# The up part of the expert tiles as three products of rounded parts, with the weights split ahead of time by GpSimd

## The chip, the cores and the metric

The kernel runs on one core of one Trainium2 chip, as one launch. The metric is the device time in microseconds, the median of three runs. The profile comes from one execution of its own; times in it are counted from the first instruction.

## The reference

A model of eight stages works on 1,024 tokens with 256 columns each. Each stage adds its result, computed from the layer-normed tokens, to the stream `x`. All values are fp32.

```python
x = x + L0_attn_a(ln(x))   # stage 0: recurrent attention in segments, 16 heads
x = x + L0_ffn(ln(x))      # stage 1: experts and a shared part, 704 wide
x = x + L0_attn_b(ln(x))   # stage 2: causal attention, 16 heads of 128
x = x + L0_ffn(ln(x))      # stage 3: weights of stage 1
x = x + L1_attn_a(ln(x))   # stage 4
x = x + L1_ffn(ln(x))      # stage 5: experts and a shared part, 176 wide
x = x + L1_attn_b(ln(x))   # stage 6
x = x + L1_ffn(ln(x))      # stage 7: weights of stage 5

def ffn(x):                # E = 8 experts, two for each token
    w, chosen = top_k(softmax(x @ gate_w.T), 2)
    y = sum(w_e * ((silu(x @ gate_e) * (x @ up_e)) @ down_e) for the two chosen e)
    return y + shared(x)   # silu(x @ g) * (x @ u) @ d
```

The inner width of an expert is 176.

## The kernel before

Tokens lie on the partitions, 128 in a tile, and `res.x` holds the stream for the whole launch. The stages follow one another, each with its own buffers and its own program for each of the five engines; nothing of a stage begins before the stage ahead of it has ended on all engines. What an engine does in a stage is an order written out by hand, with waits on semaphores.

**Products in fp32.** There are two kinds. A plain `matmul` of fp32 operands shows as two records of TensorE. `product` takes both operands as a rounded part `hi` (type float32r, made by a copy) and a rest `lo` (value minus `hi`), and adds up three matmuls, hi x hi, hi x lo and lo x hi, one record each. The shared parts, the router and the projections use `product`; the expert tiles use plain matmuls.

**An expert stage** (`ffn_stage`). After the norm and the routing, which gives every token its two experts and places, 23 tiles (`TILES`) of 128 rows each are gone through; each tile belongs to one expert, whose number TensorE's sequencer reads (`find_owner`, line 558). SP loads the weights of all 8 experts at the start of the stage, in 8 DMAs of 128 rows with 1,216 columns: 704 for the gate and up part, and 512 for the down part, of which 88 rows are used. In stages 1 and 3, three of the six loads of shared weights are queued behind them. For each tile:

- GpSimd gathers 128 rows of the normed tokens (`gather`, line 384), 8 tiles ahead, and scatters the result (`scatter`, line 391). Its order is 8 gathers, then scatter i and gather i+8 in turn.
- TensorE: `turn_x` transposes the rows (514), `expert_up` multiplies them by the 352 gate and up columns, in two halves of 128 rows of weights (527), `turn_h` transposes h (538), `expert_down` multiplies it by the down part (551).
- ScalarE copies the transposed rows (`x_out`, 659), applies silu (665), copies the transposed h (`h_out`, 671) and the result (`y_out`, 677).
- VectorE multiplies silu by the up part (`h_of_tile`, 882).

Before the loop VectorE works out the weights of the tokens (lines 856 to 876), in stages 5 and 7 with a diagonal matrix of weights (872); in stages 1 and 3 it also adds a first run of the shared part (`add_shared`). After the loop TensorE does the rest of the shared part, SP waits for the last scatter and loads the scattered rows back, and VectorE adds them.

The order on TensorE in the loop is, for tile i: `turn_x(i+3)`, `find_owner(i+2)`, `expert_up(i+2)`, `expert_down(i)`, `turn_h(i+1)`.

**GpSimd in stages 0 and 2.** Both stages go over four groups of four heads. GpSimd splits the weights of a group in hi and lo: a copy by adding zero (lines 2645 and 1055) and a subtraction (2648 and 1058), 128x1024 each. In stage 0 (`recurrent_stage`) it splits seven such blocks at the start of a group and is then idle until TensorE has done the group's output products. In stage 2 (`wide_stage`) the splits of a group are spread over the group; those of the output weights wait for TensorE's output products.

## Time and profile before

| | us |
|---|---|
| median of three runs | 1646.33 |
| lowest and highest | 1643.37, 1650.38 |
| span of the profiled execution, first to last instruction | 1607.0 |
| device time of the profiled execution | not listed; the runs lie 36 to 43 above its span |
| TensorE busy in it | 1491.0 (93%) |
| VectorE busy | 909.4 (57%) |
| ScalarE busy | 752.9 (47%) |
| GpSimd busy | 412.6 (26%) |

TensorE's granted clock was full nearly throughout (mean 0.995). The stages begin at about 0 (stage 0), 416 (1), 549 (2), 953 (3), 1085 (4), 1241 (5), 1345 (6) and 1499 us (7). In the views, PE is TensorE, PEld its weight loads, PEldq its sequencer, DVE is VectorE, ACT ScalarE, POOL GpSimd, and SPq or POOLq a queue that issues DMAs. The time of a matmul record includes its passage through the pipeline, so the cost of one in a row of many is the distance between two starts. L527 is line 527 of the kernel. A row of windows gives the stretch, its length, the busy time and count of PE, PEld, DVE, ACT and POOL, the granted clock, the DMA share and the GB/s.

### The profile page before, as it was taken

The numbers are of one execution on the slowest core, as the hardware profiler recorded it, in microseconds if no ns is written. First come the engines' busy times: TensorE is split into PE (matmuls) and PEld (weight loads), VectorE is DVE, ScalarE is ACT, GpSimd is POOL, SyncE is SP. The second block draws the span as 40 slices with busy tenths as digits, with TensorE's granted clock in tenths as the row PEclk, the third lists the DMA queues.
The fourth block names the chain that finished last, engine by engine and source line by source line (L and its number), as shares of the span: only waits on it lengthen the run. The fifth ranks groups of instructions, "written<-read, shape, count | busy, mean of one in ns | idle before, by whom it ended". The sixth has DMA issues, their size and how long they took to land. (4 is left out here: it accounts for less than half of the span.)

```text
span 1607.0 us, 28561 instructions
## 1 busy us (share of the span) xinstructions
PE 1491.0 (93%) x10462; PEld 1100.8 (68%) x10462; DVE 909.4 (57%) x1972; ACT 752.9 (47%) x1872; POOL 412.6 (26%) x328
## 2 busy tenths in 40 slices
PE   6999999998899899999999999998998998999898
PEld 4778877777677677778777767765555676533576
DVE  5766576666651656566565557147665515477712
ACT  5564656655334334343434433433443343677242
POOL 2706125040136142031211012622000461100173
PEclk9999999999999999999999999999999999999999
DMA  4103010010513421000010024221000523000533
GB/s 152 37 1 92 2 66 28 21 33 2 221 44 96 162 59 47 1 13 33 13 33 0 1 84 165 86 93 48 2 1 24 209 92 114 1 1 1 188 100 124
DMA packets 43143, 99.99 MB, mean 62 GB/s; under 512 B 7184, under 2 KB 21904, under 8 KB 42896
## 3 DMA queue, kind: packets, MB, share of 16 engines
q1 hardware_dynamic: 33040, 70.05, 12.9%
q0 software_dynamic: 9984, 28.32, 5.4%
q8 instruction: 79, 1.29, 0.3%
q14 instruction: 40, 0.33, 0.1%
HBM read 80.00 MB, written 18.35 MB: 61 GB/s over the span
## 5 line engine op out<-in xcount | busy, mean ns | idle before, releaser
L882 DVE TENSOR_TENSOR s_h_e<-s_bank,s_silu_e 128x176 f32<-128x176 f32 x92 | 31.2, 341 | 182.1 <-ACT s_silu_e L665 182.1
L527 PE MATMUL s_bank<-s_expert_w,s_xe 128*128 x368 | 124.8, 462 | 1.8 <-ACT s_xe L659 1.1
L384 POOL DMA_INDIRECT s_xg<-normed_rows,s_from_row x92 | 93.1, 1011 | 106.8 <-DVE s_from_row L790 79.9
L144 POOL TENSOR_SCALAR ln_var<-ln_moments 128x4 f32<-128x4 f32 x16 | 4.1, 255 | 450.7 <-DVE ln_moments L129 261.7
L391 POOL DMA_INDIRECT expert_rows<-s_y,s_to_row x92 | 91.1, 990 | 89.5 <-ACT s_y L677 71.5
L2645 POOL TENSOR_TENSOR s_w_hi<-s_w_raw,zero 128x1024 fp32r<-128x1024 f32 x25 | 55.6, 2222 | 211.0 <-PE s_memory L80 188.0
L1251 ACT ACTIVATE s_scratch<-s_bank,s_neg_max 128x128 f32<-128x128 f32 (+3 forms) x128 | 67.3, 528 | 84.9 <-DVE s_neg_max L1341 84.7
L551 PE MATMUL s_bank<-s_expert_w,s_he 88*128 x368 | 95.4, 381 | 4.9 <-ACT s_he L671 4.9
L1341 DVE TENSOR_REDUCE s_neg_max<-s_bank 128x1 f32<-128x128 f32 (+3 forms) x128 | 59.5, 487 | 55.9 <-PE s_bank L1141 55.7
L1139 PE MATMUL s_bank<-s_k,s_q 128*128 128x128 f32 (+3 forms) x256 | 88.6, 441 | 1.5 <-DVE s_v L1336 0.8
L551 PEld LDWEIGHTS s_bank<-s_expert_w,s_he 88*128 88x128 f32 x368 | 69.1, 189 | 29.7 <-issue 6.9
L1055 POOL TENSOR_TENSOR s_w_hi<-s_w_raw,zero 128x1024 fp32r<-128x1024 f32 x11 | 22.7, 2060 | 254.6 <-PE s_bank L80 122.8
L2331 ACT ACTIVATE s_exps<-s_bank,s_rms 128x512 f32<-128x512 f32 x128 | 76.7, 696 | 19.9 <-PE s_bank L2211 19.9
L78 PE MATMUL s_bank<-xn_t_hi,s_w_hi 128*128 128x512 f32 x192 | 80.9, 421 | 1.3 <-DVE xn_t_lo L211 1.2
L527 PEld LDWEIGHTS s_bank<-s_expert_w,s_xe 128*128 128x128 f32 x368 | 62.7, 190 | 22.6 <-issue 3.2
L1158 PE MATMUL s_bank<-s_probs_t,s_v 128*128 128x512 f32 (+3 forms) x256 | 74.6, 434 | 1.7 <-ACT s_probs_t L1259 1.7
L80 PE MATMUL s_bank<-xn_t_hi,s_w_lo 128*128 128x512 f32 x192 | 75.7, 394 | 0.0
L79 PE MATMUL s_bank<-xn_t_lo,s_w_hi 128*128 128x512 f32 x192 | 75.6, 394 | 0.0
L1259 ACT ACTIVATE s_probs_t<-s_bank 128x128 f32<-128x128 f32 (+3 forms) x128 | 49.0, 438 | 52.4 <-PE s_bank L1152 52.4
L86 PE MATMUL s_bank<-zeros 128*128 128x512 bf16 x256 | 64.0, 392 | 9.3 <-PEq L254 3.9
L1351 DVE TENSOR_SCALAR s_scratch<-s_scratch,s_row_sum 128x128 f32<-128x128 f32 (+3 forms) x128 | 67.8, 529 | 4.5
L1158 PEld LDWEIGHTS s_bank<-s_probs_t,s_v 128*128 128x128 f32 x256 | 47.5, 189 | 30.5 <-issue 17.2
(398 smaller groups left out, 4291.0 us busy)
## 6 DMA issues: line engine op xcount, KB each, us to landing
s_expert_w<-in_experts SPq DMA_DIRECT2D x32, 608.0 KB, 13.5
s_w_raw<-in_wa_o SPq DMA_DIRECT2D x16, 512.0 KB, 3.5
s_yg<-expert_rows SPq DMA_DIRECT2D x32, 256.0 KB, 4.3
s_raw<-in_shared SPq DMA_DIRECT2D x16, 384.0 KB, 6.1
normed_rows<-s_ln_xn POOLq DMA_DIRECT2D x8, 512.0 KB, 9.5
s_w_raw<-in_wa_k SPq DMA_DIRECT2D x4, 512.0 KB, 3.8
s_w_raw<-in_wa_v SPq DMA_DIRECT2D x4, 512.0 KB, 3.5
s_w_raw<-in_wa_q SPq DMA_DIRECT2D x4, 512.0 KB, 4.3
```

The source lines that it names most:

```text
L78: pe.matmul(out, sh, mh, start=first, stop=False, skip_group_check=True)
L79: pe.matmul(out, sh, ml, start=False, stop=False, skip_group_check=True)
L80: return pe.matmul(out, sl, mh, start=False, stop=last, skip_group_check=True)
L384: pool.indirect_dma_start(out=xg[:, i % XG_RING, :], out_offset=None, in_=x_rows[:, :], in_offset=bass.IndirectOffsetOnAxis(ap=from_row[:, ...
L391: pool.indirect_dma_start(out=y_rows[:, :], out_offset=bass.IndirectOffsetOnAxis(ap=to_row[:, i:i + 1].bitcast(U32), axis=0), in_=y[:, i % ...
L527: last = pe.matmul(u_bank[i % 2][:, 0:2 * INTER], xe[:, i % 2, x], expert_of(P, i, w), start=c == 0, stop=c == DC - 1, skip_group_check=True)
L551: last = pe.matmul(y_bank[i % 2][:, 0:D], he[0:IHALF, i % 2, h], expert_of(IHALF, i, w), start=c == 0, stop=c == 1, skip_group_check=True)
L1139: pe.matmul(to, q[:, b, h * S + r * P:h * S + (r + 1) * P], k[:, b, h, 0:(r + 1) * P], start=r == UNIT_ROWS[u][0], stop=False, skip_group_ ...
L1158: last = pe.matmul(o_bank[:, j * P:S], v[:, b, j, h * DH:(h + 1) * DH], probs_t[:, j, j * P:S], start=j == 0, stop=j == TB - 1, skip_group ...
L1251: act.activation(probs[:, h % 2, r, 0:(r + 1) * P], score_bank(h, r), ACT.Exp, bias=neg_max[:, 4 * h + r:4 * h + r + 1], accum_out=row_sum ...
L1351: dve.tensor_scalar(mine, mine, one, None, ALU.mult).then_inc(probs_done, 1)
L2331: act.activation(exps[:, s % 2, g, :], s_bank[g][:], ACT.Exp, scale=rms[:, b, 1, j:j + 1]).then_inc(exp_done, 1)
```

## The change

The up part of an expert tile becomes `product`, with rounded parts of the transposed rows (`xe_hi`, copied by ScalarE, and `xe_lo`, subtracted by VectorE in `low_x`) and of the expert's weights. The down part stays a plain matmul. The expert weights' parts come from DRAM: a new class `ExpertSplit` lets GpSimd load a piece of the weights, split it, and store both parts, in stage 0 for stages 1 and 3 (16 pieces of 352 columns, four behind each group's own splits), and in stage 2 for stages 5 and 7 (8 pieces of 704 columns, two before the loop over the groups and two in each of three groups ahead of the split of the output weights; that loop is written out now). Each expert stage then loads three blocks for each expert, hi, lo and the down part, in 24 DMAs. The order of TensorE, ScalarE and VectorE in the loop is changed: transposes of the rows run four tiles ahead, the up part three. Some buffers share addresses now (`first_of`).

```diff
@@ ffn_stage @@
-        e = sb("expert_w", [P, N_EXP, EXP_COLS])
+        e_hi, e_lo = sb("expert_w_hi", [P, N_EXP, EXP_DOWN], F32R), sb("expert_w_lo", [P, N_EXP, EXP_DOWN], F32R)
+        e_down = sb("expert_w_down", [IHALF, N_EXP, 2 * D])
...
+        xe_hi, xe_lo = sb("xe_hi", [P, 2, D], F32R), sb("xe_lo", [P, 2, D], F32R)
...
                     for one in range(N_EXP):
-                        sp.dma_start(e[:, one, :], experts[one]).then_inc(e_loaded, 16)
+                        for to, part in zip((e_hi, e_lo), experts[1:]):
+                            sp.dma_start(f32(to[:, one, :]), part[one]).then_inc(e_loaded, 16)
+                        sp.dma_start(e_down[:, one, :], experts[0][one, 0:IHALF, EXP_DOWN:EXP_COLS]).then_inc(e_loaded, 16)
...
             def expert_up(i):
-                pe.wait_ge(xe_done, i + 1)
+                pe.wait_ge(xe_lo_done, i + 1)
...
-                    last = pe.matmul(u_bank[i % 2][:, 0:2 * INTER], xe[:, i % 2, x], expert_of(P, i, w),
-                                     start=c == 0, stop=c == DC - 1, skip_group_check=True)
+                    last = product(pe, u_bank[i % 2][:, 0:2 * INTER], (xe_hi[:, i % 2, x], xe_lo[:, i % 2, x]),
+                                   [part_of(part, i, w) for part in (e_hi, e_lo)], c == 0, c == DC - 1)
...
             turn_x(2)
             expert_up(1)
+            turn_x(3)
             turn_h(0)
+            find_owner(2)
+            expert_up(2)
             for i in range(TILES):
-                if i + 3 < TILES:
-                    turn_x(i + 3)
-                if i + 2 < TILES:
-                    find_owner(i + 2)
-                    expert_up(i + 2)
-                expert_down(i)
+                if i + 4 < TILES:
+                    turn_x(i + 4)
                 if i + 1 < TILES:
                     turn_h(i + 1)
+                expert_down(i)
+                if i + 3 < TILES:
+                    find_owner(i + 3)
+                    expert_up(i + 3)
...
@@ scalar @@
             for i in range(TILES):
-                if i + 3 < TILES:
-                    x_out(i + 3)
                 if i + 2 < TILES:
                     silu_of(i + 2)
-                y_out(i)
+                if i + 4 < TILES:
+                    x_out(i + 4)
                 if i + 1 < TILES:
                     h_out(i + 1)
+                y_out(i)
...
@@ vector @@
+            def low_x(i):
+                dve.wait_ge(xe_hi_done, i + 1)
+                dve.tensor_tensor(xe_lo[:, i % 2, :], xt_bank[i % 2][:, 0:D], f32(xe_hi[:, i % 2, :]), ALU.subtract).then_inc(xe_lo_done, 1)
+
+            low_x(0)
+            low_x(1)
             if early:
                 for b in range(4):
                     add_shared(b, 1)
+            h_of_tile(0)
+            low_x(2)
+            h_of_tile(1)
+            low_x(3)
             for i in range(TILES):
-                h_of_tile(i)
+                if i + 2 < TILES:
+                    h_of_tile(i + 2)
+                if i + 4 < TILES:
+                    low_x(i + 4)
...
@@ wide_stage, gpsimd @@
-            with pool.Fori(1, GROUPS) as i:
-                split(i, (0, 1, 2))
+            if by_run:
+                for n in range(2):
+                    expert_split.piece(pool, n, n, 0, n == 0)
+            for i in range(1, GROUPS):
+                split(i, (0, 1))
+                if by_run:
+                    for n in range(2):
+                        expert_split.piece(pool, 2 * i + n, 2 * i + n, 0)
+                split(i, (2,))
                 move_q(i)
+            if by_run:
+                expert_split.end(pool, N_EXP)
...
@@ recurrent_stage, gpsimd @@
-            groups(pool, group)
+            for G in range(GROUPS):
+                group(G, G < GROUPS - 1)
+                for n in range(4 * G, 4 * G + 4):
+                    expert_split.piece(pool, n, n // 2, n % 2 * E_PART, n == 0)
+            expert_split.end(pool, 2 * N_EXP)
...
+class ExpertSplit:
...
+    def piece(self, pool, n, expert, at, first=False):
...
+        if not first:
+            pool.wait_ge(self.stored, 32 * n)
+        pool.dma_start(f32(self.lo[:]), of(self.experts)).then_inc(self.loaded, 16)
+        pool.wait_ge(self.loaded, 16 * n + 16)
+        pool.tensor_tensor(self.hi[:], f32(self.lo[:]), self.res.zero[:].broadcast_to([P, self.columns]), ALU.add).then_inc(self.hi_done, 1)
+        pool.wait_ge(self.hi_done, n + 1)
+        pool.tensor_tensor(self.lo[:], f32(self.lo[:]), f32(self.hi[:]), ALU.subtract).then_inc(self.lo_done, 1)
+        pool.dma_start(of(self.parts[0]), f32(self.hi[:])).then_inc(self.stored, 16)
+        pool.wait_ge(self.lo_done, n + 1)
+        pool.dma_start(of(self.parts[1]), f32(self.lo[:])).then_inc(self.stored, 16)
```

## Rows read from the trace of the kernel before

**Rows 1.** Timeline of TensorE, stage 1: start, us, engine, line, out<-in, count
```profile
486.30 1.35 PE L527 MATMUL s_bank<-s_expert_w,s_xe 128*128 x4
487.48 1.03 PE L551 MATMUL s_bank<-s_expert_w,s_he 88*128 x4
488.35 0.38 PE L538 MATMUL s_bank<-ident,s_h_e 128*88 128x128 f32 x2
...
488.79 1.35 PE L527 MATMUL s_bank<-s_expert_w,s_xe 128*128 x4
```

**Rows 2.** Groups by line, 480 to 505: count | busy us, mean ns | idle before
```profile
L677 ACT ACTIVATE s_y<-s_bank 128x256 f32<-128x256 f32 x10 | 3.8, 384 | 5.5 <-PE s_bank L551 5.5
...
L882 DVE TENSOR_TENSOR s_h_e<-s_bank,s_silu_e 128x176 f32<-128x176 f32 x10 | 3.4, 342 | 21.5 <-ACT s_silu_e L665 21.5
```

**Rows 3.** Timeline of GpSimd, stage 1, with idle time before and its releaser
```profile
474.28 1.01 POOL L391 DMA_INDIRECT expert_rows<-s_y,s_to_row  x1 [19.23 <-ACT s_y L677]
475.59 0.96 POOL L384 DMA_INDIRECT s_xg<-normed_rows,s_from_row  x1 [0.30 <-issue]
476.85 1.00 POOL L391 DMA_INDIRECT expert_rows<-s_y,s_to_row  x1 [0.30 <-ACT s_y L677]
...
527.76 0.97 POOL L391 DMA_INDIRECT expert_rows<-s_y,s_to_row  x1 [0.99 <-ACT s_y L677]
```

**Rows 4.** Timeline of TensorE in stages 1 and 2, products of rounded parts
```profile
446.32 0.39 PE L80 MATMUL s_bank<-xn_t_hi,s_w_lo 128*128 128x512 f32 x1
446.55 0.39 PE L78 MATMUL s_bank<-xn_t_hi,s_w_hi 128*128 128x512 f32 x1
...
638.23 0.28 PE L78 MATMUL s_bank<-xn_t_hi,s_wq_hi 128*128 x1
...
638.94 1.02 PE L1139 MATMUL s_bank<-s_k,s_q 128*128 128x512 f32 x2
```

**Rows 5.** Line 558, reading of a tile's owner: ns min/median/max, first and last start
```profile
L558 PEldq TENSOR_LOAD <-s_owner x92: 294/300/541, 463.5 to 1579.6; - x92
```

**Rows 6.** DMA issues of the page: count, KB each, median us to landing
```profile
normed_rows<-s_ln_xn POOLq DMA_DIRECT2D x8, 512.0 KB, 9.5
...
s_xg<-normed_rows,s_from_row POOLq DMA_INDIRECT x92, 2.8
```

**Rows 7.** Timelines of TensorE, VectorE and GpSimd at the loop's start, stage 7
```profile
1526.62 1.38 PE L527 MATMUL s_bank<-s_expert_w,s_xe 128*128 x4
...
1527.98 1.22 DVE L872 TENSOR_TENSOR s_weight_diagonal<-ident,s_token_w 128x1024 f32<-128x1024 f32 x1
...
1528.13 1.90 POOL L384 DMA_INDIRECT s_xg<-normed_rows,s_from_row  x1 [0.30 <-issue]
```

**Rows 8.** SP's queue in stage 1; busy time by windows (DMA, GB/s last), stage 7
```profile
418.76 4.82 SPq L359 DMA_DIRECT2D s_expert_w<-in_experts  x8
...
1518.00:1520.00 2.00, 0.64 (x10) 0.36 (x10) 1.91 (x2) 0.00 (x0) 0.00 (x0) 1.00 1.02 423
```

**Rows 9.** Timeline of ScalarE, stage 1, rounding of a later load of shared weights
```profile
446.79 0.83 ACT L619 ACTIVATE s_w_hi<-s_raw 128x768 fp32r<-128x768 f32 x1
```

**Rows 10.** Timeline of GpSimd, stage 0, first split of a group
```profile
134.39 1.89 POOL L2645 TENSOR_TENSOR s_w_hi<-s_w_raw,zero 128x1024 fp32r<-128x1024 f32 x1 [64.01 <-PE s_memory L80]
136.36 2.41 POOL L2648 TENSOR_TENSOR s_w_lo<-s_w_raw,s_w_hi 128x1024 fp32r<-128x1024 f32 x1
```

**Rows 11.** Line 3009 of VectorE: ns min/median/max; windows of two splits, stage 2
```profile
L3009 DVE SCALAR_TENSOR_TENSOR s_sigma_kt<-s_exp_part,s_positive x32: 668/692/716, 23.3 to 314.2; 128x512 f32<-128x512 f32 x32
L3009 DVE SCALAR_TENSOR_TENSOR s_sigma_qt<-s_exp_part,s_positive x32: 676/1509/2719, 39.8 to 350.4; 128x512 f32<-128x512 f32 x32
...
613.00:618.00 5.00, 3.58 (x14) 1.91 (x12) 4.93 (x6) 1.16 (x4) 4.24 (x2) 1.00 0.00 0
709.00:714.00 5.00, 5.00 (x22) 3.28 (x21) 4.14 (x7) 1.51 (x4) 4.41 (x2) 1.00 0.00 0
```

More of the change, by code:

```diff
@@ L36 @@
 XG_RING, Y_RING = 8, 8
+E_PART = EXP_DOWN // 2
 AT_ORDER = P
@@ L256, in ffn_stage, with first_of @@
         sb = lambda what, shape, dt=F32: ctx.enter_context(nc.sbuf_tensor(f"{name}_{what}", shape, dt))
+        def first_of(what, shape):
+            with nc.sbuf_tensor(f"{name}_{what}", shape, F32) as first:
+                return first
         banks = [ctx.enter_context(nc.psum_tensor(f"{name}_bank{i}", [P, HALF], F32)) for i in range(8)]
@@ L3147, in _, with __init__, end @@
             groups(dve, group)
+class ExpertSplit:
+    def __init__(self, nc, ctx, sem, name, res, experts, parts, columns):
+        sb = lambda what, dt: ctx.enter_context(nc.sbuf_tensor(f"{name}_{what}", [P, columns], dt))
+        self.res, self.experts, self.parts, self.columns = res, experts, parts, columns
+        self.hi, self.lo = sb("e_hi", F32R), sb("e_lo", F32R)
+        self.loaded, self.hi_done, self.lo_done, self.stored = (
+            sem("e_raw_loaded"), sem("e_hi_done"), sem("e_lo_done"), sem("e_stored"))
+    def piece(self, pool, n, expert, at, first=False):
+        cols = slice(at, at + self.columns)
+        of = lambda whole: whole[bass.ds(expert, 1), :, cols].rearrange("a p n -> (a p) n")
+        if not first:
[8 more added lines that the diff above has]
+        pool.dma_start(of(self.parts[1]), f32(self.lo[:])).then_inc(self.stored, 16)
+    def end(self, pool, n):
+        pool.wait_ge(self.stored, 32 * n)
 class Residual:
@@ L3207, in build_program @@
         t = {**t, "x_mid": nc.dram_tensor("x_mid", (SEG, SEGS // 2, 2, B, D), F32, kind="Internal").ap()}
+        for n in range(2):
+            t[f"experts{n}_parts"] = [nc.dram_tensor(f"experts{n}_{part}", (N_EXP, P, EXP_DOWN), F32, kind="Internal").ap()
+                                      for part in ("hi", "lo")]
         rows = [nc.dram_tensor("normed_rows", (TOK, D), F32, kind="Internal").ap(),
@@ L3216, in build_program @@
             if kind == "L0_ffn":
-                ffn_stage(nc, name, res, t["shared0"], t["experts0"], t["gate0"], t["routing"], rows, True, False, "both" if n > 1 else "moments", None)
+                ffn_stage(nc, name, res, t["shared0"], [t["experts0"], *t["experts0_parts"]], t["gate0"], t["routing"], rows, True, False, "both" if n > 1 else "moments", None)
             if kind == "L0_attn_b":
@@ L3224, in build_program @@
             if kind == "L1_ffn":
-                ffn_stage(nc, name, res, t["shared1"], t["experts1"], t["gate1"], t["routing"], rows, False, True, "both" if n > 1 else "", out if n == len(stages) - 1 else None)
+                ffn_stage(nc, name, res, t["shared1"], [t["experts1"], *t["experts1_parts"]], t["gate1"], t["routing"], rows, False, True, "both" if n > 1 else "", out if n == len(stages) - 1 else None)
         nc.clear_and_free_semaphores(Semaphores.past.pop())
```

35 lines of the change are left out of this document (19 added, 16 removed).

## The prediction

> **What bounds the kernel now.** I read the timeline of TensorE inside an expert loop first, because all that the change can speed up lies there. There are four such loops (stages 1, 3, 5 and 7), of 23 tiles each. The reader sees one tile after another with no idle time on TensorE: up part from 486.30 to 487.48 (1.18 us), down part to 488.35 (0.87), the two pairs of transposes to 488.79 (0.44), and the next up part begins [rows 1]. So a tile costs 2.49 us, and TensorE alone sets it: ScalarE has four instructions of at most 384 ns in that time, VectorE one of 342 ns [rows 2]. The second engine to look at is GpSimd: in its timeline scatter, gather and scatter start at 474.28, 475.59 and 476.85, that is 2.57 us for a pair [rows 3]. That is more than a tile of TensorE; it does not bind only because 8 gathers are made ahead, so that 15 pairs and then 8 single scatters are left. From the first to the last scatter are 527.76 - 474.28 = 53.5 us.
>
> **The up part.** Two plain products of 352 columns show now as four matmul records, 0.295 us each. They become six products of rounded parts. No row shows rounded parts at 352 columns, but there are rows on both sides: 512 columns start 0.23 us apart, 256 columns 0.118 (six of them from 638.23 to 638.94) [rows 4]. Between them 352 columns give 0.16 us, six 0.96 us. The rows at 256 columns are addressed through a loop register, as the expert's weights are, so the address costs nothing there. Bounds: 0.95 (in proportion to 512 columns) and 1.18 (nothing gained). I take 0.96: 0.22 us less in a tile, 2.27 us. TensorE's sequencer also reads the owner of a tile (300 ns) [rows 5], now behind the down part; that part's eight queued instructions hide it. Uncovered it would cost 0.3 us in a tile.
>
> **The new order.** The transposes run four tiles ahead and the up part three, so every wait inside an iteration is for work of the iteration before. At the end of the loop the last down parts then follow each other directly: 0.96 + 0.22 + 0.87, then 1.09, then 0.87, which is 4.0 us for the last three tiles.
>
> **But GpSimd then ends last.** First to last scatter cannot take less than 15 pairs of 2.57 and 7 singles of 1.3: 47.7 us. TensorE alone would take 19 tiles of 2.27 and those 4.0: 47.1. The gathers add a little. A gather lands 2.8 us after its issue [rows 6], so gather i+8 is there 1.3 + 2.8 + 2.57 i after the first scatter's start. TensorE asks for it at 7.2 + 2.27 i (four tiles, 9.1, less the 1.9 from that transpose through down part and copy to a scatter). At i = 14 it comes 1.1 us late. I take 48.0 us from first to last scatter: 5.5 us less in a stage, 22.0 in four. Bounds: 6.4 (TensorE alone) and 4.7 (both delays in full).
>
> **The rounded x.** VectorE gets one subtraction of 256 columns in a tile. It reads one operand from PSUM, as the 342 ns product of 176 columns does; an estimate from that is 0.4 us. VectorE is then busy for 0.75 of 2.27 us. Queued behind the subtraction's wait for ScalarE is the product h of the next tile, which TensorE needs an iteration later: no cost inside the loop. At its start there is one. In stages 5 and 7 the first subtraction stands behind the whole weighting of the tokens, which ends with the diagonal at 1527.98 + 1.22 = 1529.2; now the first up part runs at 1526.62 [rows 7]. It will start 3.0 us later. Part of this comes back: three up parts are shorter by 0.22, and GpSimd's early gathers, one of them 1.90 us long [rows 7], now still hold TensorE there. Bounds 0.7 and 3.0; I take 1.4, nearer to the lower, as the following tiles will find their gathers landed. In stages 1 and 3 two subtractions stand ahead of the adding of the shared part: 0.25 each, between 0 and 0.8. Together 3.3 us.
>
> **The loads.** 8 DMAs of 608 KB become 24 of together 7,040 KB, 2.23 MB more. SP issues 8 in 4.82 us, so 24 take 14.5; transfers ran at 423 GB/s up to 1520 [rows 8], so the last part lands 5.3 us later, at about 1525.4. From there to the first subtraction (owner, transpose, copy) is some 1.5 us, 1526.9: hidden behind the same 1529.2. If it lands after 1527.7, each microsecond is lost twice (stages 5 and 7). In stages 1 and 3 the loads of more shared weights are queued behind on SP; the first now goes out at 418.76 + 14.5 = 433.2, lands by 442.7 even with the slowest landing below, and ScalarE takes it at 446.79 [rows 9]. Hidden.
> The Trainium skill (DMA: Bandwidth & Descriptors, section "Why a DMA increments its semaphore by 16 and not by 1") says that a DMA is spread over the largest number of engines up to 16 that divides its rows, so the down parts with 88 rows would use 11. No row here shows such a DMA. By that rule eleven engines carry 0.49 MB each instead of 0.31, and the last part lands at an estimated 1527.0, which leaves the sum as it is, with 0.7 us of cover.
>
> **The splitting on GpSimd.** 16 pieces in stage 0, 8 in stage 2. A piece is three DMA issues, two landings one after another (load, then the stores before the next piece), a rounding copy and a subtraction. At 1024 columns those two take 1.89 and 2.41 us [rows 10]; in proportion 1.5 us for 352 columns, 3.0 for 704. A landing takes between 2.8 us (a gather) and 9.5 (the normed rows, stored by GpSimd while the experts load) [rows 6]. With three issues of about 0.9 a piece is between 10 and 23 us; I take 11, as little else is loaded in stage 0. Four pieces, 44 us, lie in a gap of 64.0 us [rows 10]: hidden. Behind them on GpSimd are the next group's splits, needed half a group later.
> What is not hidden is that GpSimd and VectorE hinder each other. The same instruction of VectorE takes 692 ns as sigma_k, when GpSimd is idle, and 1509 (median) as sigma_q, when GpSimd splits [rows 11]. From 613 to 618, while GpSimd split, TensorE was busy for 3.58 of 5 us; from 709 to 714, in the same split, for all 5 [rows 11]. The new pieces are 24 us of such work in each of the two stages. Bounds: 0, and 8 (1.42 lost for each 4.24 us of splitting, all through stage 2) plus 6 in stage 0, 14. I take 2, as most stretches are like the later one.
> The Trainium skill (GPSIMD Engine Reference, section "Specifications") says that the two engines share SBUF interfaces, with contention for VectorE instructions in a two-port mode or with two SBUF inputs. The trace agrees (1509 against 692 ns). By that rule the splits pay, and the new subtraction, with one input in PSUM, leaves the gathers alone; this speaks for the 2 us and against the second rival.
>
> **The sum.** -22.0 + 3.3 + 2 = -16.7 us. The profiled execution's span goes from 1607.0 to 1590.3. Its own device time is not listed; the three runs lie 36 to 43 us above its span, the median 39.3, and nothing in the change touches that part. So 1646.3 - 16.7 = 1629.6, about **1630 us**. Unchanged means within 0.5%, 1638.1 to 1654.6.
>
> **The rivals.**
> *The splits collide with the attention stages.* The 3.58 of 5 us speak for it, the later stretch against. At 8 to 14 us instead of 2 the time is 1636 to 1642. Chance 0.10.
> *The gathers collide with the new subtraction*; this one ends slower. A gather issued beside VectorE's late work took 1.90 us instead of 0.96 [rows 7, 3]. If each pair of the loop took x more, GpSimd would set the loop at 47.7 + 15 x. From x = 0.39 the loop gains nothing; at the 0.94 seen it takes 61.8, 8.3 us more than now, four times, with the 5.3 on top: 1685 us. Against it: the h product of today, also with one operand in PSUM, runs beside pairs of 2.57 us. Chance 0.04.
> *The pieces overrun stage 0.* Decides from 16 us a piece, when four no longer fit into the 64.0. At 23 us each gap is overrun by 28; the last one has nothing behind it that could absorb it: 1658 us. Chance 0.03.
> *The weights land late in stages 5 and 7.* Decides at 1527.7. At 1530 it costs 2.3 us twice: 1634. No row shows loads in 88 rows of 2 KB, so 0.08.
> *The six products are little faster than the four*, since each weight load of about 190 ns shows: 1.14 in a tile, 50.7 in the loop, 1641 us. Against it stand the 0.118 us of [rows 4], with a load for each. Chance 0.03.
> My forecast has 0.72, between 1622 and 1637.
>
> **How the numbers follow.** 1630 is the forecast's own. The range 1621 to 1641 takes in the loop at its best (-25.6 + 1.4, no collisions: 1622), the late weights, the last rival and most of the first; outside are the second, the third and the worst of the first. Faster by over 0.5%: 0.72 + 0.08 + a third of the first rival, 0.83. Unchanged: the rest of that and the last rival, 0.10. Slower: the second and third, 0.07.
>
> **What would show it.** Right: a tile of 2.27 us with an up part of 0.96; near 48 us from first to last scatter; the first up part of stage 7 some 3 us behind its place; no wait of stage 0 for a split. Wrong: an up part near 1.14; pairs over 2.9 us; TensorE waiting for the expert weights; stages 0 and 2 longer by more than 4 us together.

## The result, and the profile after

The changed kernel takes 1667.78 us (median of four runs, 1662.52 to 1675.05) against 1646.07 us for the kernel before; the ratio is 1.0135, with a 95% interval of 1.0104 to 1.0167. It is slower by 21.7 us, where the prediction had it 16.7 us faster.

The first thing to read is the cores' view. It gives the span and the mean granted clock of TensorE, here of the kernel after and then of the kernel before run once more (its device time was 1649.98 us):

```profile
core 0: 1665.8 us, clock 0.974
```

```profile
core 0: 1648.2 us, clock 0.993
```

Device time and span lie 1.7 to 1.8 us apart. The span of 1607.0 that stood ahead of the prediction came from an execution some 37 us quicker than those timed, and of the 39 us that the prediction took to lie between span and device time, all but 1.8 lie inside the span of a usual execution. So the profile after is compared below with the second profile of before, the usual one.

**The tile on TensorE** [rows 1], in the timeline of the kernel after, stage 1:

```profile
502.08 1.03 PE L561 MATMUL s_bank<-s_expert_w_down,s_he 88*128 x4
502.75 0.51 PE L79 MATMUL s_bank<-s_expert_w_hi,s_xe_hi 128*128 x1
503.10 0.33 PE L80 MATMUL s_bank<-s_expert_w_lo,s_xe_hi 128*128 x1
...
503.75 0.32 PE L81 MATMUL s_bank<-s_expert_w_hi,s_xe_lo 128*128 x1
503.91 0.38 PE L525 MATMUL s_bank<-ident,s_xg 128*128 128x128 f32 x2
504.13 0.38 PE L549 MATMUL s_bank<-ident,s_h_e 128*88 128x128 f32 x2
504.35 1.03 PE L561 MATMUL s_bank<-s_expert_w_down,s_he 88*128 x4
505.03 0.51 PE L79 MATMUL s_bank<-s_expert_w_hi,s_xe_hi 128*128 x1
506.17 0.38 PE L525 MATMUL s_bank<-ident,s_xg 128*128 128x128 f32 x2
508.29 0.42 PE L549 MATMUL s_bank<-ident,s_h_e 128*88 128x128 f32 x2 [1.74 <-issue]
510.93 2.07 PE L561 MATMUL s_bank<-s_expert_w_down,s_he 88*128 x4 [2.22 <-ACT s_he L684]
513.09 0.49 PE L80 MATMUL s_bank<-s_expert_w_lo,s_xe_hi 128*128 x1
513.38 0.49 PE L81 MATMUL s_bank<-s_expert_w_hi,s_xe_lo 128*128 x1
```

One tile takes 504.35 - 502.08 = 2.27 us, the predicted number. The products are 0.16 us apart. But from 506.17 on TensorE stands still for most of 5 us, and then the products are 0.29 us apart: the granted clock was at half (1.2 GHz) from 509.2 to 516.0. What was missing is seen on ScalarE (timeline, idle time before each instruction in brackets):

```profile
503.29 0.39 ACT L690 ACTIVATE s_y<-s_bank 128x256 f32<-128x256 f32 x1 [0.58 <-PE s_bank L561]
507.54 0.32 ACT L678 ACTIVATE s_silu_e<-s_bank 128x176 f32<-128x176 f32 x1 [3.87 <-PE s_bank L81]
508.98 0.38 ACT L672 ACTIVATE s_xe_hi<-s_bank 128x256 fp32r<-128x256 f32 x1 [1.12 <-remote]
510.41 0.38 ACT L684 ACTIVATE s_he<-s_bank 88x256 f32<-88x256 f32 x1 [1.04 <-remote]
```

The silu at 507.54 waited for the up part that TensorE had ended at 503.75 + 0.32 = 504.07. Its semaphore was raised at 507.52, 3.4 us late; that of the transposes begun at 503.91 at 508.96, 4.7 us after their end, and that of the transposes of h behind them at 510.39, 5.9 us after theirs. In the execution of 1607.0 us the signals that ScalarE waits for in the loops are all raised within 0.02 us of the end. TensorE meanwhile went on to the next tile until it needed ScalarE's answer. So TensorE's work was on time and its signals were not. There are such places in every expert loop of every usual execution, the kernel before included, and none in the execution of 1607.0 us. The same rows as [rows 3], line of the scatters (ns min/median/max, first and last start), stage 1, after and then before in its second profile:

```profile
L402 POOL DMA_INDIRECT expert_rows<-s_y,s_to_row x23: 968/997/1011, 480.4 to 538.6; - x23
```

```profile
L391 POOL DMA_INDIRECT expert_rows<-s_y,s_to_row x23: 970/997/1010, 474.0 to 535.3; - x23
```

That is 58.2 us from first to last scatter after, 61.3 before, where the execution of [rows 3] had 53.5 and the prediction 48.0. The loop did get shorter. What got longer is the way to it. Busy time by windows in stage 7 after (the last three numbers are clock, DMA share and GB/s), to be held against the 423 GB/s of [rows 8]; below them TensorE and VectorE at the loop's start [rows 7]:

```profile
1558.00:1560.00 2.00, 1.39 (x14) 0.80 (x15) 1.36 (x7) 0.00 (x0) 0.00 (x0) 1.00 1.05 324
1564.00:1566.00 2.00, 0.00 (x0) 0.00 (x0) 1.79 (x9) 0.00 (x0) 1.69 (x2) 1.00 0.83 248
1568.00:1570.00 2.00, 0.00 (x0) 0.00 (x0) 0.00 (x0) 0.00 (x0) 1.62 (x2) 0.50 0.76 263
1574.00:1576.00 2.00, 0.57 (x2) 0.29 (x2) 0.00 (x0) 0.00 (x0) 0.00 (x0) 0.50 0.03 12
```

```profile
1566.62 1.23 DVE L886 TENSOR_TENSOR s_weight_diagonal<-ident,s_token_w 128x1024 f32<-128x1024 f32 x1
1575.43 0.66 PE L525 MATMUL s_bank<-ident,s_xg 128*128 128x128 f32 x2 [12.06 <-DMA s_expert_w_down<-in_experts]
1576.54 0.42 DVE L901 TENSOR_TENSOR s_xe_lo<-s_bank,s_xe_hi 128x256 fp32r<-128x256 f32 x1 [8.69 <-ACT s_xe_hi L672]
```

The diagonal behind which the subtraction was to stand is done at 1567.85. The weights land at 1574.1 (the end of their last packet; all landings are read so), and TensorE waits 12.06 us for them; the loop then begins at half the clock. From 12 us after the start of the stage on, all loads ran at some 330 GB/s, the last ones at 250. In stages 1 and 3 the shared weights queued behind the expert weights went out at 440.57 instead of the estimated 433.2, and TensorE waited for them (7.0 us in the page, behind the rest `s_w_lo`: 2.3 in stage 1 and 4.7 in stage 3).

Where the usual spans part, from the timelines (SP's first load of a stage is its start):

| kernel, stages 1 / 3 / 5 / 7 | first scatter after the start, us | first to last scatter, us |
|---|---|---|
| before, span 1607.0 | 57.8 / 56.6 / 34.3 / 34.8 | 53.5 / 53.5 / 52.9 / 53.5 |
| before, usual, 1648.2 | 57.7 / 56.1 / 34.5 / 34.7 | 61.3 / 62.6 / 63.1 / 64.2 |
| after, 1665.8 | 62.5 / 63.1 / 45.1 / 46.6 | 58.2 / 58.2 / 58.3 / 61.5 |

The loops gave 15.1 us back in all, the later starts cost 34.3, stage 0 cost 1.7; the rest of the 17.6 us is -3.3.

### The profile page after: what moved, and what is told of

It reads as the page before. It is cut to its first block and busy times, and to the rows that moved or that the text cites. A ratio compares the mean times of both kernels' runs of the same rounds, so it can differ in the third digit from the quotient of the medians.

```text
span 1665.8 us, 29369 instructions
## 1 busy us (share of the span) xinstructions
PE 1502.3 (90%) x10646; PEld 1139.7 (68%) x10646; DVE 942.6 (57%) x2064; ACT 752.7 (45%) x1872; POOL 502.8 (30%) x448
## 5 line engine op out<-in xcount | busy, mean ns | idle before, releaser
L561 PE MATMUL s_bank<-s_expert_w_down,s_he 88*128 x368 | 102.3, 404 | 10.2 <-ACT s_he L684 8.9
L1380 DVE TENSOR_REDUCE s_neg_max<-s_bank 128x1 f32<-128x128 f32 (+3 forms) x128 | 59.6, 487 | 55.8 <-PE s_bank L1180 55.6
L79 PE MATMUL s_bank<-s_expert_w_hi,s_xe_hi 128*128 x184 | 78.1, 425 | 3.3 <-DVE s_xe_lo L901 3.3
L561 PEld LDWEIGHTS s_bank<-s_expert_w_down,s_he 88*128 88x128 f32 x368 | 66.5, 201 | 20.2 <-issue 13.1
L1933 DVE TENSOR_REDUCE s_neg_max<-s_pair 128x2 f32<-128x1024 f32 (+3 forms) x64 | 51.5, 821 | 25.0 <-PE s_pair L1707 24.2
```

The costliest lines, as they stand in the source:

```text
L79: pe.matmul(out, sh, mh, start=first, stop=False, skip_group_check=True)
L561: last = pe.matmul(y_bank[i % 2][:, 0:D], he[0:IHALF, i % 2, h], part_of(e_down, i, slice(c * D, (c + 1) * D)), start=c == 0, stop=c == 1, ...
```

## The experiments

**The kernel before again**, unchanged.

> The kernel before once more, unchanged, to see where its device time and its span part. The prediction took the 39 us between the span of 1607.0 us and the median of 1646.3 as something that lies around the span. In the trace of the changed kernel the span (1665.8) and the device time (1667.5) are 1.7 us apart, so that reading is in doubt. Theory: a usual execution of the kernel before has a span of about 1644 us, and the 37 us more than in the profile shown are in the four expert loops, as waits for signals of TensorE that come late (first to last scatter 60 us or more instead of 53.5). Rival: the span is 1607 again, the loops take 53.5, and 39 us lie outside the span.

Device time 1649.98, span 1648.2. The four loops take 37.9 us more than in the first profile, of 41.2 us in the span. The theory holds: what the prediction counted as lying outside is time inside the loops, behind late signals; in the first profile none of them is late.

**The splitting alone**: the kernel before with the pieces of `ExpertSplit` in stages 0 and 2; `ffn_stage` is that of before.

```diff
+    for n in range(4 * G, 4 * G + 4):
+        expert_split.piece(pool, n, n // 2, n % 2 * E_PART, n == 0)
+expert_split.end(pool, 2 * N_EXP)
```

> The kernel before with the splitting of the expert weights by GpSimd in stages 0 and 2 added and nothing else: the parts are stored, but the expert stages load and use the plain weights as before. Theory (the cost of the change lies in the expert stages): 0 to 4 us above the kernel before. Rival (the splits collide with the attention stages): 8 to 14 us above it. In the two traces at hand stage 0 grew by 1.5 us and stage 2 shrank by 3.1.

1652.07 us, ratio 1.0001 (0.9979 to 1.0024). It costs nothing that can be measured; the interval, 3.5 us less to 4.0 us more, shuts out the rival, but not the 2 us of the prediction.

**The loads alone**: the kernel before with three loads for each expert and plain products.

```diff
-    sp.dma_start(e[:, one, :], experts[one])...
+    for to in (e_up, e_again):
+        sp.dma_start(to[:, one, :], experts[one][:, 0:EXP_DOWN])...
+    sp.dma_start(e_down[:, one, :], experts[one][0:IHALF, EXP_DOWN:EXP_COLS])...
```

> The kernel before with the 24 loads of the changed kernel instead of its 8: the columns of the up part are loaded twice (into two tiles; the second is not used) and the down part in 88 rows, and the products stay plain, in the order of before. Theory (the loads cost what the loop gained): the weights land 10 us later than the loop of before needs them in stages 5 and 7, and the late loads of shared weights cost some us in stages 1 and 3: 20 to 30 us above the kernel before. Rival (late signals inside the loop, or the rounded parts, cost the time): 0 to 8 us above it.

1673.08 us, ratio 1.0125 (1.0085 to 1.0164). First scatters 59.6, 59.1, 47.1 and 47.6 us after the starts, loops as before. The loads alone cost about what the whole change does.

**Down parts over 128 rows.**

```diff
-    e_down = sb("expert_w_down", [IHALF, N_EXP, 2 * D])
+    e_down = sb("expert_w_down", [P, N_EXP, 2 * D])
-    sp.dma_start(e_down[:, one, :], experts[0][one, 0:IHALF, EXP_DOWN:EXP_COLS])...
+    sp.dma_start(e_down[:, one, :], experts[0][one, :, EXP_DOWN:EXP_COLS])...
```

> The changed kernel, but the down part of each expert is loaded over 128 partitions instead of 88 (the 40 added rows are not used). In stages 5 and 7 the weights of the changed kernel land at about 1295 and 1574 us, 34 us after SP's first load of them. Theory 1 (a load of 88 rows uses 11 of the 16 DMA engines, which end last): the last part lands 3 to 5 us earlier in each stage, and the time falls by 6 to 10 us, to about 1659. Theory 2 (it is the bytes and the short rows of 2,816 and 2,048 bytes, moved at 332 instead of 423 GB/s, that make the loads late): 0.7 MB more are moved, the last part lands where it did or up to 1 us later, and the time is 1666 to 1672.

1648.43 us, ratio 0.9974 (0.9953 to 0.9994): all of the loss is gone, though 0.7 MB more are moved in each expert stage. By the two ratios that is some 26 us; the medians lie only 19 apart, but they were taken beside runs of the kernel before that differ by 6. In stages 5 and 7 the weights land 29.8 and 30.0 us after the start instead of 34.3 and 35.6, and in stages 1 and 3 the first scatter is back at 58.3 and 56.8. In stage 7 a window 21 us after the start has 413 GB/s, where the one of the kernel after had 324:

```profile
1545.00:1547.00 2.00, 2.00 (x11) 0.93 (x10) 1.87 (x7) 0.74 (x2) 0.55 (x1) 1.00 1.05 413
```

The direction is that of theory 1; the gain is well above the 6 to 10 us that it named, so its reason needed a test of its own.

**96 rows**, a number that 16 divides.

```diff
-    sp.dma_start(e_down[:, one, :], experts[0][one, 0:IHALF, EXP_DOWN:EXP_COLS])...
+    sp.dma_start(e_down[:, one, :], experts[0][one, 0:96, EXP_DOWN:EXP_COLS])...
```

> The changed kernel with the down part loaded over 96 partitions: more rows than the 88 of the change by 8, but a number that 16 divides. In the changed kernel the 8 loads of 88 rows left 40 small packets fewer than the 128-row loads (568 against 608 in the same stretch), which is 11 instead of 16 for each load. Theory (the number of DMA engines that a load is spread over makes the difference): as the 128-row loads or slightly sooner, weights landed 30 us after the start of stages 5 and 7, 1645 to 1651. Rival (the number of rows, and the share of partitions that are written, makes it): near the 88 rows, 34 to 35 us, 1660 to 1668.

1668.46 us, ratio 1.0085 (1.0057 to 1.0113); landed after 35.8 and 34.6 us. Stage 7 of the kernel after, of 128 and of 96 rows, in the DMA view:

```profile
DMA packets 4347, 10.58 MB, mean 278 GB/s; under 512 B 568, under 2 KB 696, under 8 KB 4344
```

```profile
DMA packets 4707, 11.24 MB, mean 296 GB/s; under 512 B 608, under 2 KB 736, under 8 KB 4704
```

```profile
DMA packets 4451, 10.71 MB, mean 282 GB/s; under 512 B 608, under 2 KB 736, under 8 KB 4448
```

The 40 small packets fewer fit 8 loads of 88 rows spread over 5 engines less each; with 96 rows none is missing. Yet with 96 rows the weights of stages 5 and 7 land as late. So the number of engines is not the cause of the late landing: theory 1 falls. (The time is some 14 us above the kernel before by its ratio, between the two others: in stage 1 the first scatter comes after 58.6 us, not 62.5.) What goes with the landing is the duration of a packet: in stage 7 those of 2,816 bytes took 118 ns on average beside 128-row loads, 136 beside 88 rows, 146 beside 96.

**No down loads, and down loads last.** In the first the down product takes other columns of the loaded weights; in the second the order of SP's loads alone is changed (the diff is the second's).

```diff
     for one in range(N_EXP):
         for to, part in zip((e_hi, e_lo), experts[1:]):
             sp.dma_start(f32(to[:, one, :]), part[one])...
+    for one in range(N_EXP):
         sp.dma_start(e_down[:, one, :], experts[0][one, 0:IHALF, EXP_DOWN:EXP_COLS])...
```

> The changed kernel with the loads of the down part left out: the down products take other columns of the loaded weights, so the output is not the reference's. What the two parts of the up weights take by themselves: 5.8 MB. Theory (partial loads, of 88 or 96 of 128 rows, slow the packets of the loads beside them: the mean packet of 2,816 bytes took 118 ns beside 128-row loads, 136 beside 88 rows, 146 beside 96): packets of 118 ns or less, the weights land 24 to 26 us after the start of stages 5 and 7, and 8 loads of 88 rows cost about 10 us where their bytes are worth 4; the time is 1636 to 1645. Rival (the many 2,816-byte loads are slow by themselves): packets of 130 ns and more, 28 us and later, 1645 to 1655.

> The changed kernel with its 88-row loads, but all 16 loads of the up parts go first and the 8 down parts after them. Theory (the partial loads slow what runs beside them): the up parts land by 26 us, the 88-row loads alone after them by 31 to 32, and the time is 1648 to 1657. Rival (the 88 rows cost the same in any order, as 11 engines carry them): 34 to 36 us and 1660 to 1668.

Windows of stage 7, without down loads and then with them last:

```profile
1545.00:1547.00 2.00, 2.00 (x10) 1.40 (x10) 1.73 (x9) 1.57 (x3) 0.00 (x0) 1.00 1.04 406
1549.00:1551.00 2.00, 0.64 (x13) 0.46 (x13) 1.81 (x2) 0.00 (x0) 0.00 (x0) 1.00 1.04 415
```

```profile
1549.00:1551.00 2.00, 1.31 (x20) 0.83 (x19) 1.39 (x4) 0.00 (x0) 0.00 (x0) 1.00 1.04 413
1555.00:1557.00 2.00, 0.00 (x0) 0.00 (x0) 1.86 (x7) 0.00 (x0) 1.69 (x2) 1.00 0.79 267
```

By themselves the loads of the parts run at 406 to 415 GB/s, with packets of 117 ns in both runs; the 88-row loads alone run at about 260. The landing is at 24.4 us without them and at 31.0 with them last, instead of 35.6 mixed in. So the partial loads slow the loads beside them, as the theory had it. The times are 1647.45 us (ratio 0.9995, 0.9970 to 1.0020) and 1658.01 (1.0046, 1.0016 to 1.0075), the first 2 us and the second 1 us above the bounds named. The second hangs on one run of ten that took 2839.64 us; without it the median is 1656.7, inside. As to the first: without down loads the weights are no longer last, and the loop of stages 5 and 7 waits for the rounded x. There the first up part runs 30.0 us after the start against 27.1 in the usual run of before, the 3.0 us later that the prediction had, and the first scatter is 3.8 to 4.3 us later. TensorE in stage 7, without down loads:

```profile
1560.59 0.65 PE L79 MATMUL s_bank<-s_expert_w_hi,s_xe_hi 128*128 x1 [2.37 <-DVE s_xe_lo L899]
```

The Trainium skill (DMA: Bandwidth & Descriptors, section "The descriptor swizzle") says that in a transfer to 128 partitions each engine writes one port of SBUF; for other shapes it points to the rule for the number of engines. A guess from that is that with 88 or 96 rows engines write to ports that other engines use too, beside the full loads; the 136 and 146 ns against 118 would fit, but no run shows the ports.

**Longer rows**: the two parts side by side in memory (5,632-byte rows), and then the down part copied beside them too (7,680-byte rows, one load for each expert); the diff is the first's.

```diff
-    for to, part in zip((e_hi, e_lo), experts[1:]):
-        sp.dma_start(f32(to[:, one, :]), part[one])...
+    sp.dma_start(f32(e_parts[:, one, :]), experts[1][one])...
```

> As the run with 128-row down loads, and besides the two parts of the up weights stand side by side in memory and come in one load of 5,632-byte rows for each expert (16 loads instead of 24, the same bytes). Theory (short rows move at 332 GB/s, the 4,864-byte rows of before at 396 to 423): the last weights land some 3 us earlier in each expert stage, about 27 us after the start of stages 5 and 7 instead of 30, and the time is 1636 to 1643. Rival (the number of bytes and what else is stored and gathered then set the landing, not the rows): the landing stays at 30 us and the time at 1646 to 1651.

> As the run before, and the down part too is copied beside the two parts while the experts are split (one more DMA of GpSimd, memory to memory, for each expert), so that 8 loads of 7,680-byte rows bring all weights. Theory (rows): another 1 to 2 us earlier in each expert stage, 1630 to 1640 in all. Rival: no earlier than in the run before, or the copies make stages 0 and 2 longer; 1640 to 1650.

1648.62 and 1648.38 us (ratios 1.0019, 1.0003 to 1.0036, and 1.0003, 0.9984 to 1.0022); landed after 29.6 and 29.4 us. The rivals hold: with 128 rows the length of a row is worth half a microsecond.

**The order alone**, with plain products; ScalarE's order goes with it. The diff gives the calls for tile i in their order, without the code around them.

```diff
-    turn_x(i + 3), find_owner(i + 2), expert_up(i + 2), expert_down(i), turn_h(i + 1)
+    turn_x(i + 4), turn_h(i + 1), expert_down(i), find_owner(i + 3), expert_up(i + 3)
```

> The kernel before with the new order alone (transposes four tiles ahead, the up part three); the products stay plain, nothing is split, the loads are those of before. Theory (the new order lets more of a late signal pass unseen): the loops take 58 to 61 us instead of 61 to 64, some 10 us less in all, about 1640. Rival (the gain of the changed loop is that of the shorter up part): the loops stay at 61 to 64 us, within 4 us of the kernel before.

1641.53 us, ratio 0.9971 (0.9948 to 0.9994). The loops take 59.5, 58.2, 60.4 and 59.2 us, 14.1 less in all than usual, where the whole change gave 15.1: in loops with late signals the order gives the gain, and the shorter up part next to nothing. Each number is of one execution; over the seven runs that have the change's products, order and gathers, with the ring of 8, the four loops take 236 to 244 us together, here 237. The time fell by less than the loops, by 4.8 us (1.0 to 8.6). In this profile the part of the span behind the loop of stage 3 is 4.7 us longer than in the usual one, with 13.7 us at 1.2 GHz from 1121.2 on.

**No gathers inside the loop**, once for the changed kernel with 128-row loads and once for the kernel before.

```diff
     for i in range(TILES):
         scatter(i)
-        if i + XG_RING < TILES:
-            gather(i + XG_RING)
```

> As the run with 128-row down loads, but the 15 gathers inside each expert loop are left out: tiles 8 to 22 take the rows that were gathered for an earlier tile. In usual executions the signals of TensorE come up to 3.4 us late while gathers and scatters are under way, in the kernel before as in the changed one (first to last scatter 61 to 64 and 58 to 61 us, against the 53.5 of the one execution that the prediction had). Theory (GpSimd's DMAs delay the signals, and without the gathers TensorE alone is left): 47 us from first to last scatter in each loop, about 1600 us in all. Rival 1 (the delay has nothing to do with the gathers): 58 to 61 us as before, 1646 to 1651. Rival 2 (only GpSimd's pairs of 2.57 us are taken away, the scatters still delay signals): 52 to 56 us, 1620 to 1635.

> The kernel before without the 15 gathers inside each expert loop (tiles 8 to 22 take rows gathered for earlier tiles, so the output is not the reference's). The changed kernel without them took 47.4 us from first to last scatter in every loop. Theory (then TensorE alone sets both loops, and the three products with the new order are worth 6 us in each): 53 to 54 us here, and some 1612 to 1622 us in all. Rival (the loop of before is held by something else as well): over 56 us.

1600.66 us (ratio 0.9716, 0.9694 to 0.9739) and 1612.75 (0.9773, 0.9739 to 0.9806). The scatters of stage 1, changed and before:

```profile
L402 POOL DMA_INDIRECT expert_rows<-s_y,s_to_row x23: 968/969/1010, 475.2 to 522.7; - x23
```

```profile
L391 POOL DMA_INDIRECT expert_rows<-s_y,s_to_row x23: 969/969/1007, 473.8 to 527.3; - x23
```

47.4 us in all four loops, and 53.5, 53.5, 53.0 and 53.5: what TensorE alone takes, and for the kernel before, to 0.1 us, the loops of the 1607.0 us execution. Of the 92 signals for ScalarE in a loop, 18 to 34 came over 0.5 us late in the usual execution of before, in the kernel after, in the one with 128-row loads and in the one with the new order; here there are none, but for two of up to 1.0 us in stage 5 of the second run.

**A ring of 16 tiles**, so that 16 gathers are made ahead and 7 inside the loop, in the changed kernel with 128-row loads and in the kernel before.

```diff
-XG_RING, Y_RING = 8, 8
+XG_RING, Y_RING = 16, 8
```

> The changed kernel with 128-row down loads and a ring of 16 gathered tiles instead of 8: 16 gathers are made ahead of the loop and 7 inside it. Theory (pairs of gather and scatter on GpSimd make TensorE's signals late and set the loop; the loop without gathers took 47.4 us): the loops take 47 to 51 us instead of 58 to 62, and the time is 1605 to 1620. Rival 1 (what counts is that GpSimd has DMAs under way at all, and the same 23 gathers are only moved): the loops gain less than 4 us, 1635 to 1650. Rival 2 (the first scatter now stands behind 16 gathers on GpSimd, and stages 5 and 7, where the gathers can begin only 22 us after the stage, give back what the loop gains): 1620 to 1635.

> The kernel before with the ring of 16 gathered tiles and nothing else. Theory: its loops fall from 61 to 64 us to the 53.5 us that TensorE alone takes for plain products, or up to 56, and the time is 1608 to 1625. Then the three products of the changed kernel are worth what its loops take less (6 us each), against weights that land later. Rival (the kernel before is held by TensorE, not by late signals): its loops stay above 60 us, 1640 to 1652.

1653.11 us (ratio 1.0014, 0.9998 to 1.0030) and 1670.39 (1.0110, 1.0090 to 1.0130), above all that was expected of either. The loops do fall, to 51.2 to 53.7 and 56.6 to 60.2 us, but the first scatter comes later by 7 to 8 us in the changed kernel and by 7 to 12 in the other. Moving the gathers moves their cost: in stages 1 and 3 of the changed kernel the first up part itself is 7.7 and 8.4 us later, as signals of TensorE come late while the 16 gathers are issued (one raised at 466.12 in stage 1 lies 7 us behind the last product that can have raised it), and in stages 5 and 7 the first scatter stands behind 16 gathers on GpSimd.

**Plain loads in place of the 15 gathers**, by SP and then by GpSimd, in the changed kernel with 128-row loads.

```diff
-    pool.indirect_dma_start(out=xg[:, i % XG_RING, :], in_=x_rows[:, :], in_offset=...)...
+    pool.dma_start(xg[:, i % XG_RING, :], x_rows[i % NT * P:(i % NT + 1) * P, :])...
```

> The changed kernel with 128-row down loads; inside the loop the 15 gathers of GpSimd are replaced by as many plain loads of SP, of the same 128 rows x 1 KB each into the same ring, but of fixed rows of the stored tokens, so the output is not the reference's. Without any gather in the loop it took 47.4 us from first to last scatter, with them 58 to 62. Theory (it is GpSimd's gathers, not the loading as such, that make TensorE's signals late): 47 to 50 us, about 1600 to 1612 us in all. Rival (any DMA that loads beside the scatters does it): 56 us and more, 1635 to 1650.

> The same, but the plain loads of fixed rows are issued by GpSimd, in the places of the 15 gathers (the output is not the reference's). Theory A (the indirect addressing of the gathers matters): 47 to 51 us from first to last scatter, 1600 to 1615 in all. Theory B (that GpSimd's queue moves them matters): 56 us and more, 1635 to 1650.

1596.27 and 1603.51 us (ratios 0.9684, 0.9657 to 0.9710, and 0.9729, 0.9695 to 0.9762); every loop takes 47.4 us in both. The scatters of stage 1 in the second, and GpSimd between two of them:

```profile
L405 POOL DMA_INDIRECT expert_rows<-s_y,s_to_row x23: 972/1002/1010, 475.9 to 523.3; - x23
```

```profile
489.49 1.00 POOL L405 DMA_INDIRECT expert_rows<-s_y,s_to_row  x1 [0.70 <-ACT s_y L693]
490.49 0.56 POOL L396 DMA_DIRECT2D s_xg<-normed_rows  x1
491.75 1.00 POOL L405 DMA_INDIRECT expert_rows<-s_y,s_to_row  x1 [0.69 <-ACT s_y L693]
```

So neither the loading nor GpSimd's queue as such delays the signals; the indirect DMAs do. But a plain load also takes GpSimd 0.56 us, not the 0.97 of a gather, and leaves it idle for 0.7 us in each tile, where gathers and scatters follow without a break. So these runs do not tell whether it is the gather, or any indirect DMAs that are issued without a break; the next ones bear on that.

**The rows sorted ahead**: 16 scatters of the normed tokens to their places, after which SP loads every tile as a plain block; with the three products and 128-row loads, and then in the kernel before.

```diff
-    for i in range(XG_RING):
-        gather(i)
+    for j in range(ROWS):
+        pool.indirect_dma_start(out=x_rows[:, :], out_offset=..., in_=norm.xn[:, j % NT, :])...
...
+    for i in range(TILES):
+        sp.dma_start(xg[:, i % XG_RING, :], x_rows[i * P:(i + 1) * P, :])...
```

> The changed kernel with 128-row down loads, and no gather at all: before the loop GpSimd scatters the normed tokens to their places among the tiles' rows (16 scatters of 128 rows, straight from the normed tokens), and SP loads each tile as a plain block of 128 rows; rows of a tile that belong to no token hold finite left-over values, as nobody reads their results. The output is the reference's. Theory (only indirect gathers make TensorE's signals late): the loops take 47 to 48 us. The 16 scatters (1.3 us each, 21 us) must all have landed before the first tile: in stages 5 and 7 the loop begins 6 to 10 us later than the 33.5 us of the run with 128-row loads, in stages 1 and 3 where it did. 1603 to 1622 us. Rival (scatters while TensorE works on the shared part make signals late too, or the later start eats the gain): 1630 to 1648.

> The kernel before with the same sorting of the tokens instead of gathers; products, order and weights as before. Theory: the loops take the 53.5 us that TensorE needs, and begin some 14 us later than the kernel before in stages 5 and 7: 1630 to 1645 us, so that the three products of the rounded parts, worth 6 us in each loop and with their late weights now hidden behind the scatters, make the run above 20 to 25 us faster than this one. Rival (the products are worth nothing in time, as in the loops with gathers): within 8 us of the run above.

1637.59 us, ratio 0.9930 (0.9902 to 0.9958), and 1657.69, ratio 1.0081 (1.0053 to 1.0110). The scatters of the results, stage 1:

```profile
L395 POOL DMA_INDIRECT expert_rows<-s_y,s_to_row x23: 958/958/961, 481.7 to 528.5; - x23
```

```profile
L384 POOL DMA_INDIRECT expert_rows<-s_y,s_to_row x23: 958/959/961, 478.3 to 531.3; - x23
```

Every loop takes 46.8 or 46.9 us with the three products and 53.0 without. The first scatters in stages 5 and 7 come at 52.2 to 52.5 us in both, so the late weights cost nothing here. The run with the products is faster than both kernels, and has the lowest median of those that leave nothing out; from the order alone (0.9971) its interval does not part it. Its time is the rival's all the same, some 16 us above the theory's bound: the later start eats much of the gain, in stages 1 and 3 too (7 us there). The run without them is 13 us above its bound for the same reason. The difference of the two medians, 20.1 us (25 by the ratios), is what the change, with 128-row loads, is worth once TensorE's signals come on time inside the loops and its loads are hidden.

The other half of the rival is seen too. Ahead of the loop, while GpSimd issues the 16 scatters, TensorE's signals are late again (run with the products, stage 1):

```profile
451.26 0.96 POOL L402 DMA_INDIRECT normed_rows<-s_ln_xn,s_place  x1 [0.30 <-issue]
452.52 0.96 POOL L402 DMA_INDIRECT normed_rows<-s_ln_xn,s_place  x1 [0.30 <-issue]
454.34 0.28 PE L81 MATMUL s_bank<-s_w_hi,s_h_lo 128*128 128x256 f32 x1
458.85 0.96 POOL L402 DMA_INDIRECT normed_rows<-s_ln_xn,s_place  x1 [0.30 <-issue]
462.15 0.85 ACT L626 ACTIVATE s_w_hi<-s_raw 128x768 fp32r<-128x768 f32 x1 [5.73 <-remote]
```

The rounding on ScalarE at 462.15 waited for the product that ended at 454.62; its signal was raised at 462.13, 7.5 us late. The run without the products shows the same at the same place, also 7.5 us. So it is not the gather alone: indirect scatters that follow each other every 1.27 us delay the signals as well, and one scatter in 2.0 to 2.5 us, as in most of the loop here, does not.

## Why the prediction was wrong, step by step

- **The up part, right.** 2.27 us a tile and products 0.16 apart, as read between the rows of 512 and 256 columns. Without gathers the loop took 47.4 us; the prediction had 47.1 for TensorE alone.
- **The 39.3 us between span and median, of which "nothing in the change touches that part", wrong.** The difference was late signals in the very loops that the change speeds up. The loop of before was not set by TensorE in a usual execution, so a shorter tile could hardly shorten it. Instead of -22.0 us the loops gave -15.1, and the order alone gives -14.1. Whether GpSimd would end last at 48.0 us was not tested: with on-time signals there was no run of the new products with gathers in the loop.
- **The loads, "hidden", wrong; this decides the sign.** The step that failed was 423 GB/s for all bytes, read from 128-row loads. With the 88-row loads among them the loads ran at some 330 and then 250 GB/s and landed 35.6 us after the start of stage 7 instead of 25.9; with 128-row loads it was still 30.0. The rival of late weights had the place and the mechanism, and its price of 4 us was too small: the later starts cost 34.3 us over the four stages, and with the loads alone they cost 30.4. The stages 1 and 3, called hidden by their raw loads, are 11.8 of it.
- **The rule of the Trainium skill that I weighed** (DMA: Bandwidth & Descriptors, section "Why a DMA increments its semaphore by 16 and not by 1"): the 40 small packets fewer agree with 11 engines for 88 rows. The estimate drawn from it, 1.6 us, was far too small, and the 96 rows show that the number of engines is not what costs.
- **The rounded x, right in its place.** Where the weights did not hide it, the up part began 3.0 us later as worked out. The prediction let 1.6 of these come back; nothing did (the first scatter was 3.8 to 4.3 us later).
- **The splitting, right.** Predicted 2 us; measured none, give or take 4. A piece took 7.45 us (loads begun at 79.29 and 86.74) instead of 11. The rival of colliding splits falls.
- **The rival of gathers colliding with VectorE's subtraction, wrong.** A pair stayed at 2.58 us (scatters at 480.44 and 483.02 in stage 1). What the gathers go with is late signals of TensorE, with or without the change.
- **The clock.** The trace shows 90.0 us at 1.2 GHz after and 26.0 in the usual run of before. Of the 90.0, 10.2 and 13.7 lie behind the waits for weights in stages 5 and 7, and 6.8 in each of the four loops, behind a late signal. What that cost apart from the waits was not measured.

Left open: by what way GpSimd's indirect DMAs hold up TensorE's signals, how close together they must come to do it, and why one execution of before, with the same gathers, ran without that.

## What to carry to other kernels

Compare the span of a profile with the device times before building on it; where they part by more than a few microseconds, find the place first, as it may be the place of the change. Price loads by rows of the same shape: loads that fill 88 or 96 of 128 partitions were slow and slowed the full ones beside them, and loading unused rows was faster. Where an engine is idle for a signal, hold the end of the work against the time at which the waiting engine goes on; if the signal itself is late, shortening the work gains nothing, and what runs beside it (here GpSimd's indirect DMAs, one right behind the other) is what to take away; spreading them out was not tested.

## What the hardware showed that was not expected

- Signals of TensorE came late while GpSimd's indirect DMAs followed each other without a break: up to 3.4 us in the usual loops of before, 5.9 in those of the kernel after, and 7.5 while 16 scatters were issued one every 1.27 us. 15 gathers between the scatters cost a loop 8 to 14 us; 15 plain loads of the same size, by SP or by GpSimd, cost it nothing (47.4 us), nor did the loop's scatters by themselves.
- Loads of 2,816-byte rows to 128 partitions ran at 406 to 415 GB/s; 88-row loads by themselves at about 260; mixed, all of them at some 330, and with 128-row loads in place of the 88-row ones at 413.
